# One Exp activation over two PSUM banks for a pair of score units in a fused attention and gated feed-forward block

## What is computed

```python
q = einsum('bsd,hde->bhse', xn, wq) + bq          # xn = layernorm(x)
k = einsum('bsd,hde->bhse', xn, wk) + bk
v = einsum('bsd,hde->bhse', xn, wv) + bv
scores = softmax(einsum('bhse,bhte->bhst', q, k) / sqrt(8), axis=-1)
att = einsum('bhst,bhte->bhse', scores, v)        # heads joined, then @ wo.T + bo
x_prev = xn shifted by one token
xr, xk = mu_r * xn + (1 - mu_r) * x_prev, mu_k * xn + (1 - mu_k) * x_prev
ffn = sigmoid(xr @ W_r.T) * (square(relu(xk @ W_k.T)) @ W_v.T)
out = x + att + ffn
```

## Time and profile before

| what | value |
|---|---|
| median of 3 runs | 471.02 us (470.27 to 473.52) |
| time of the profiled execution | 472.43 us |
| its span | 469.9 us |
| mean granted clock of TensorE | 0.973 |
| DMA, mean | 129 GB/s |

### The profile page before, as it was taken

The page is one execution under the profiler, slowest core; times in us unless marked ns, Lnnn a source line. Parts: engine busy times, 40 slices in busy tenths (PEclk is TensorE's granted clock), DMA queues, the critical chain, the costliest instruction groups (busy, mean ns, idle before and its releaser), DMA issues.

```text
span 469.9 us, 15674 instructions
## 1 busy us (share of the span) xinstructions
PE 449.4 (96%) x5254; PEld 271.8 (58%) x5254; DVE 400.6 (85%) x824; ACT 390.7 (83%) x865; POOL 366.8 (78%) x674
## 2 busy tenths in 40 slices
PE   5598999999999999999999999999999999999996
PEld 4245665655666565666665656566656665666553
DVE  7478999988999999899998999899998999989831
ACT  2037989988988998988989899889998989898883
POOL 6568788888888888788888888888888888887321
PEclk9559999999999999999999999999999999999999
DMA  4543455544355454344554544355545444455100
GB/s 140 133 122 94 137 155 147 145 127 127 116 150 158 141 141 141 101 138 139 149 158 125 158 132 124 109 144 158 157 133 139 137 124 126 136 151 147 49 15 22
DMA packets 85836, 60.42 MB, mean 129 GB/s; under 512 B 6192, under 2 KB 73392, under 8 KB 85808
## 3 DMA queue, kind: packets, MB, share of 16 engines
q1 hardware_dynamic: 85808, 60.06, 45.0%
HBM read 29.89 MB, written 29.36 MB: 126 GB/s over the span
## 4 chain that ended last, share of the span: by engine, by line
PE 89%; DVE 4%; issue 2%; ACT 2%; DMA 1%; ACTq 0%; DVEq 0%; SPq 0%; POOL 0%; POOLq 0%
PE bank_val L605 26%; PE bank_exp L663 19%; PE bank_max L673 10%; PE misc L744 4%; PE misc L692 4%; PE misc L714 4%; PE misc L628 3%; PE misc L703 3%; PE misc L749 3%; PE misc L756 3%; PE misc L631 2%; DVE neg_max L533 2%; PE misc L726 2%; PE misc L721 1%; PE misc L613 1%
## 5 line engine op out<-in xcount | busy, mean ns | idle before, releaser
L533 DVE TENSOR_REDUCE neg_max<-bank_max 128x2 f32<-128x512 f32 x512 | 327.7, 684 | 41.5 <-PE bank_max L673 36.1
L434 ACT ACTIVATE probs<-bank_exp 128x512 f32<-128x512 f32 x504 | 272.9, 596 | 27.1 <-PE bank_exp L663 26.9
L673 PE MATMUL bank_max<-ops 48*128 48x256 bf16 x1024 | 164.1, 278 | 0.0
L663 PE MATMUL bank_exp<-ops 51*128 51x256 bf16 x1008 | 158.5, 273 | 4.6 <-issue 3.0
L605 PE MATMUL bank_val<-probs,val 128*25 128x256 f32 x2048 | 136.3, 384 | 1.4 <-ACT probs L434 1.4
L663 PEld LDWEIGHTS bank_exp<-ops 51*128 51x128 bf16 x1008 | 72.7, 95 | 71.6 <-issue 47.4
L605 PEld LDWEIGHTS bank_val<-probs,val 128*25 128x25 f32 x2048 | 50.4, 103 | 52.1 <-issue 26.1
L673 PEld LDWEIGHTS bank_max<-ops 48*128 48x128 bf16 x1024 | 75.1, 96 | 5.2
L344 POOL TENSOR_SCALAR xn<-x_in,moments,rstd 128x128 f32<-128x128 f32 x62 | 49.3, 803 | 0.0
L383 POOL TENSOR_TENSOR mixed_x<-mixed_x,xn_t 128x512 f32<-128x512 f32 x32 | 40.7, 1273 | 2.5
L358 POOL TENSOR_TENSOR qk_l<-qk_rest,qk_m 128x512 bf16<-128x512 f32 x31 | 36.1, 1164 | 2.5
(11 more groups left out here) (73 smaller groups left out, 619.5 us busy)
## 6 DMA issues: line engine op xcount, KB each, us to landing
ops<-spill SPq DMA_DIRECT2D x128, 192.0 KB, 3.4
spill<-qk_h SPq DMA_DIRECT2D x64, 192.0 KB, 3.4
spill<-qk_m SPq DMA_DIRECT2D x64, 128.0 KB, 1.9
x_in<-x SPq DMA_DIRECT2D x32, 128.0 KB, 2.2
spill<-qk_l SPq DMA_DIRECT2D x32, 128.0 KB, 1.8
y_out<-y SPq DMA_DIRECT2D x32, 128.0 KB, 1.9
ops<-shift SPq DMA_DIRECT2D x128, 6.0 KB
w<-weights SPq DMA_DIRECT2D x1, 448.0 KB, 3.0
```

What stands on the lines that cost most here:

```text
L434: nc.scalar.activation(probs[g % 2][:, u % G, :, :], exp_bank(u, live)[:, :, :], ACT.Exp, scale=SCALE).then_inc(exp_done[u], 1)
L533: nc.vector.tensor_reduce(out=neg_max[hf][:, :, r, pr], in_=bank_max[MAX_BANK[v]][:, :, :], axis=AX_X, op=ALU.max, negate=True).then_inc(m ...
L663: exp_mm = nc.tensor.matmul(exp_bank(u, live)[:, i, :], ops[p][rows, hf, 1, pr, i * P:(i + 1) * P], ops[p][rows, hf, 0, pr, :], start=True ...
L673: max_mm = nc.tensor.matmul(bank_max[MAX_BANK[v]][:, i, :], of[rows, max_hf, 0, max_pr, i * P:(i + 1) * P], of[rows, max_hf, 1, max_pr, :] ...
```

## The change

`bank_exp` becomes one tensor over two banks, `[P, 2, ST, S]`. Its halves are used as the two banks were. In all batches but the last (`pairs = live(1)`), ACT no longer runs an `Exp` for each unit. At an even unit it only waits; at an odd one it runs one `Exp` of 1024 columns over both halves, into two neighbouring slots of `probs`, and increments `exp_done` of the odd unit alone. PE's bank waits follow: ahead of an even unit it waits for `exp_done` of the odd unit just before it, and ahead of an odd one for none. In the last batch the exponentials stay one for each unit; PE's waits there are adapted, since `exp_done` of an even unit is counted only in that batch.

```diff
-        bank_exp = [psum(f"bank_exp{i}", [P, ST, S]) for i in range(2)]
+        bank_exp = psum("bank_exp", [P, 2, ST, S])
...
-            return bank_exp[u % 2] if live(1) or u % 4 < 2 else bank_max[u % 2]
+            return bank_exp[:, u % 2] if live(1) or u % 4 < 2 else bank_max[u % 2]
...
                     if live(0):
-                        g = u // G
+                        g, pairs = u // G, live(1)
                         act.wait_ge(exp_scores[u], n(0))
                         if u % G == 0:
                             after(act, mix_psum[(g - 2) % NG], n(0) if g >= 2 else n(-1))
-                        nc.scalar.activation(probs[g % 2][:, u % G, :, :], exp_bank(u, live)[:, :, :], ACT.Exp,
-                                             scale=SCALE).then_inc(exp_done[u], 1)
+                        if not pairs:
+                            nc.scalar.activation(probs[g % 2][:, u % G, :, :], exp_bank(u, live)[:, :, :], ACT.Exp,
+                                                 scale=SCALE).then_inc(exp_done[u], 1)
+                        elif u % 2 == 1:
+                            nc.scalar.activation(probs[g % 2][:, u % G - 1:u % G + 1, :, :], bank_exp[:, :, :, :],
+                                                 ACT.Exp, scale=SCALE).then_inc(exp_done[u], 1)
...
                         if live(1):
-                            after(pe, exp_done[(u - 2) % H], n(0) if u >= 2 else n(-1))
+
+                            if u % 2 == 0:
+                                after(pe, exp_done[(u - 1) % H], n(0) if u >= 2 else n(-1))
                         elif u < 2:
-                            pe.wait_ge(exp_done[u - 2 + H], n(-1))
+                            pe.wait_ge(exp_done[H - 1], n(-1))
                         elif u < 4:
                             pe.wait_ge(max_done[last_of_bank(u % 2)], n(0))
                         else:
-                            pe.wait_ge(exp_done[u - 4], n(0))
+
+                            pe.wait_ge(exp_done[u - 4], n(0) if u % 2 == 1 else 1)
```

More of the change, by code:

```diff
@@ L592, in keep_running @@
                 for _ in range(count):
-                    nc.tensor.matmul(bank_exp[0][:, 0, 0:P], ident[:, :], ident[:, :], start=True, stop=True)
+                    nc.tensor.matmul(bank_exp[:, 0, 0, 0:P], ident[:, :], ident[:, :], start=True, stop=True)
             def mix_values(g, count, before, parity):
@@ L667, in step @@
                             rows, of = slice(RG * r, RG * r + KS), ops[(p + ahead) % 2]
-                            nc.tensor.matmul(bank_exp[r][:, i, :], of[rows, max_hf, 0, max_pr, i * P:(i + 1) * P],
+                            nc.tensor.matmul(bank_exp[:, r, i, :], of[rows, max_hf, 0, max_pr, i * P:(i + 1) * P],
                                              of[rows, max_hf, 1, max_pr, :], start=True, stop=True)
```

## The result

The changed kernel takes 513.65 us (median of 4 runs, 511.68 to 513.85) against 472.27 us for the kernel before (median of 4, 470.27 to 474.20). The ratio is 1.0865, with a 95% interval of 1.0831 to 1.0898: slower by 41 us.

The account below looks back on a forecast made before the run. PE was taken to bound the kernel. Seven pairs stretched to 1.73 us plus 0.09 us for a late copy make a batch 0.88 us longer; 31 x 0.88 = 27.3 us on a 471.0 us median gives 498.3 us, range 488 to 514.

Parts of the forecast that it names:

- PE bounds the kernel before, ACT has slack: Steady stretch, 200 to 240 us: PE busy 39.98 of 40 us sets the rhythm; ACT has some 10% of slack.
- The wide activation: ACT's 1024-column exponential takes 1.01 us, ends 0.99 and 1.09; saves some 0.07 us a pair, alone worth nothing.
- The ring: Scores, exponential, next scores: 0.35 + 0.31 + 1.01 + 0.06 = 1.73 us, above PE's own length in seven of eight pairs.
- the second line of the ring's sum: Handover from the start of the releasing score matmul to the start of ACT's waiting exponential: 0.31 us.
- two waits instead of one on each wide activation I cost at nothing: ACT's wide exponential waits for both units' scores: no cost, since the first score is always ready earlier.
- My own upper sum: Upper end: activation of 1.09 us, 1.81 us from pair to pair, a batch 1.44 us longer, 45 us in all, 516.
- "31 batches": Batches that have pairs, each 0.88 us longer: 31 x 0.88 = 27.3 us slower.
- The `mixed` copy: ACT's copies behind unit 1 don't fit before the next exponential: 0.09 us a batch, at (2,3).
- The ring fits under PE's work: Rival: no change, 468 to 476 us, if pair-to-pair length is 1.63 us or less; chance 0.07.
- Fewer waits, faster: Rival: PE's 13.5 us of weight-load waits for exponentials are true losses and go, 457.5 us; chance 0.03.
- A longer ring: Rival: two-bank exponential costs more than both narrow ones, or copies push it; about 538 us, half 527; chance 0.07.
- The clock: PE's gaps of 0.1 us at over 90% busy should leave the granted clock at its upper level, 2.4 GHz.

Follow-up runs that it names:

- padded kernel before: Kernel before, with PE repeating one or two of its own matmuls, same result, in seven blocks of other work: 537.7 us, ratio 1.1378.
- Half of it alone: Kernel before with PE's wait alone moved: 478.6 us, ratio 1.0169; kernel before with ACT's late start alone: 472.8 us, ratio 1.0033.
- one pair alone: Kernel before, with wide activation and moved wait for one pair only: (10,11) 472.5 us, ratio 1.0010; (12,13) 479.9 us, ratio 1.0139.
- the kernel with single waits: Changed kernel, PE signalling only odd-unit scores and ACT not waiting on `mix_psum`, except in the last batch: 497.6 us, ratio 1.0538.
- with 896 columns: Changed kernel, its wide activation covering 224 of each 256 columns, the last 32 queries of each part left out: 492.5 us, ratio 1.0421.
- the kernel with the transposes in the middle: Kernel before, with the transposes behind unit 1 moved between the two halves of `mix_values(3)`: 469.95 us, ratio 0.9946.
- the kernel with the moved wait: Kernel before, PE waiting ahead of even units for the preceding odd unit's exponential, none ahead of odd; exponentials stay narrow: 478.6 us, ratio 1.0169.

## Why the prediction was right, and where its size was off

**PE bounds the kernel before, ACT has slack.** Right, and shown: the padded kernel before pays for each padded block.

**The wide activation.** Forecast 1.01 us from the starts, measured 1.024 on the mean [page of after]. ACT's instructions did save time (its busy time fell from 390.7 to 384.8 us), and it was worth nothing, as said. But it saved less than forecast: 5.9 us of busy time in all, 0.02 for each pair, where 0.07 for each pair would be 17 us. The formula of the Trainium skill (ScalarE: Activation LUTs, the section on what ACT_TABLE_LOAD costs) gives 1.04 us, so row and page are both within 0.02 us.

**The ring.** The mechanism was right in each point: seven pairs of one length, (10,11) covered, ACT waiting for PE in front of most exponentials. Half of it alone costs little, one pair alone costs by the block behind it, and in six of the seven pairs the length of the activation goes in one for one.

**The step that was mis-sized** is the second line of the ring's sum, "start of the matmul that releases it to the start of an exponential that was waiting: ... 0.31 us". It came from unit 6, an activation with one wait. I then wrote that "two waits instead of one on each wide activation I cost at nothing: the first of the two scores is always ready earlier". That was wrong, and the third wait, on `mix_psum` in four of the pairs, was not counted at all. What matters is not which score is ready earlier, but that the wait for the later one stands on a semaphore instruction ahead of the activation. The handover measured 0.36 us with two waits and 0.39 with three, so 0.08 us more in four pairs and 0.05 in two. With the additional waits taken away the kernel ran at 497.6 us, beside a forecast of 498.3.

That the time fell into the range is in part luck. My own upper sum was 516 us, for a ring of 1.81 us, and the range ended at 514. The ring did measure 1.81 us, but by the handover, for which I had allowed nothing upward, and not by a longer activation, for which the upper end stood.

The account of a batch, by the nine starts: 14.76 measured, 14.26 forecast. The handover is 4 x 0.08 + 2 x 0.05 = 0.42 us of that; the first matmuls of pairs (8,9) and (0,1) start 0.10 us after the exponential's end and not 0.06, 0.08 us together; the activation's 0.01 us in six pairs, 0.06; from it go some 0.06 us at (2,3) and in the distance to the fourth matmul (0.34 for 0.35). 31 x 0.50 = 15.5 us. The difference of 513.65 and 498.3 is 15.35, but that this agrees so closely is chance. The slowdown was forecast at 27.3 us and measured at 41.4, 14.1 apart; the rest is that the kernel before ran at 472.27 us beside it and not at 471.0. And "31 batches" times a steady batch is not the whole time. The kernel before has every fourth distance between `mixed` copies 0.3 to 0.4 us longer, where the loop turns, and some early ones more, 3.2 us in all; the changed kernel has almost nothing of that (one distance is 0.3 us longer). Mostly for that reason it is 39.0 us longer from the first to the last `mixed` copy (453.3 against 414.3), not 31 x 1.38 = 42.8; it also reaches the first one 2.5 us later. For the same reason 497.6 us is nearer to the forecast than its parts: that kernel's batch is 14.35 us, not 14.26.

**The `mixed` copy.** I added 0.09 us for it at (2,3). In the changed kernel it is not to be seen (1.79 us), because the handover by semaphores had itself grown to 0.36 us and hid it. In the kernel with single waits it is there: (2,3) lasts 1.82 us beside 1.73 for (0,1).

**The rivals.** "The ring fits under PE's work" would have needed an activation of 0.91 us or less; with 896 columns, 0.916 us, a batch was still 0.7 us longer than before, owing to the longer handover. "Fewer waits, faster" is out; the true loss by PE's waits for exponentials before was that at unit 5, and the kernel with the transposes in the middle took it away: 0.13 us in a steady batch, 2.5 us measured, not 13.5. "A longer ring" was right in that the ring was longer, by a cause that it did not name.

**The clock.** It stayed at 1.00 in the stretch from 200 to 240 us with PE busy for 37.29 of 40 us.

Open: why the first matmuls of pairs (8,9) and (0,1) start 0.04 us later than others after the exponential. These are the two that also wait for `shift_in`, and in the trace their first weight load carries that wait, issued first, where others carry the one for the exponential. It would fit that the wait for the exponential stands on an instruction of its own there too, but the trace has no record of one, and it wasn't tried apart.

## What to carry to other kernels

Before two instructions on a buffer are merged into one, write down the ring from the first write of the buffer through its reader to the next write, with both handovers, and set it beside the producer's other work for each turn. Merging saved ACT, an engine with slack, 5.9 us of busy time in all, and took away the half-buffer by which the two engines had overlapped. Where merging is wanted all the same, do it under the producer's longest block, and let the merged instruction wait on one semaphore only. Where it needs several, the traces suggest issuing first the wait that will be fulfilled last; try that before you count on it.

## What the runs showed of the hardware

- Of several semaphore waits for one activation, these traces show the one issued first on the activation and the others on semaphore instructions ahead of it. Where the last to be fulfilled was one of the others, ACT started 0.36 us after the start of the releasing matmul, or 0.39 with three waits in all; with one wait it was 0.30 (medians over the batches of four kernels with wide activations). Where the activation carried the last one itself, a second wait cost nothing: 0.31 us at unit 4 of the kernel with the moved wait. Taking the additional waits out of the changed kernel brought it from 513.65 to 497.6 us.
- An Exp over two PSUM banks costs what its columns cost: 810, 916 and 1024 ns for 768, 896 and 1024 columns; nothing extra for the second bank was seen.
- Two repeated float32 matmuls of 25 rows and 256 columns into the same partitions of a bank (four records, 0.22 us from start to start) took 0.8 us, where the 8 of a `mix_values` block (16 records), spread over four strips of partitions, take 1.0 us together. A matmul's price in a block says nothing of its price alone.
